# First attention of a two-layer decoder: projections of batches 1 to 3 from high and low parts, expert up weights loaded after them

## What is computed

```python
q = jnp.einsum('bsf,hfd->bhsd', x, wq)
k = jnp.einsum('bsf,hfd->bhsd', x, wk)
v = jnp.einsum('bsf,hfd->bhsd', x, wv)
scores = jnp.einsum('bhsd,bhtd->bhst', q, k) * scale
attn = jax.nn.softmax(scores, axis=-1)
out = jnp.einsum('bhst,bhtd->bhsd', attn, v)
feats = out.transpose(0, 2, 1, 3).reshape(x.shape[0], x.shape[1], H * DK)
return feats @ wo
...
x = x + _L0_attn_ref(_layernorm(x, axis=-1), L0_attn_wq, L0_attn_wk, L0_attn_wv, L0_attn_wo)
```

## Time and profile before

| | us |
|---|---|
| median of 3 runs | 1380.44 (1379.09 to 1383.38) |
| profiled execution | 1377.93 |
| its span, first to last instruction | 1376.0 |
| PE busy | 1247.9 (91%) |
| DVE busy | 980.6 (71%) |
| ACT busy | 710.2 (52%) |
| POOL busy | 622.6 (45%) |
| chain that ended last, on PE | 67% |

### The profile page before, as it was taken

How to read it: one execution, slowest core, us unless ns; L and a number is a source line. 1 busy time by engine, 2 the same in 40 slices (tenths; PEclk the granted TensorE clock), 3 DMA queues, 4 the chain that set the end, 5 groups by cost and what they waited for, 6 DMA issues and landing times.

```text
span 1376.0 us, 29293 instructions
## 1 busy us (share of the span) xinstructions
PE 1247.9 (91%) x10862; PEld 913.7 (66%) x10862; DVE 980.6 (71%) x2360; ACT 710.2 (52%) x1471; POOL 622.6 (45%) x770
## 2 busy tenths in 40 slices
PE   7999999999999989842669989989999999989998
PEld 5667667667776756530347656767777777777887
DVE  5988897787788778678313467677878888776554
ACT  4566666666666646510113345556666666633222
POOL 3555555555555521120631368685555755401110
PEclk9999999999999999965879989999999999999999
DMA  5131000000000020000023134211120211000001
GB/s 179 55 124 32 1 2 1 1 1 1 1 1 1 1 70 2 1 1 0 11 65 98 37 73 119 41 49 30 38 57 20 56 38 29 4 1 1 0 0 30
DMA packets 77000, 43.87 MB, mean 32 GB/s; under 512 B 26090, under 2 KB 71739, under 8 KB 76871
## 3 DMA queue, kind: packets, MB, share of 16 engines
q1 hardware_dynamic: 72390, 38.58, 10.6%
q10 hardware_dynamic: 2432, 2.28, 0.5%
q0 software_dynamic: 2048, 1.27, 0.4%
HBM read 21.89 MB, written 10.49 MB: 24 GB/s over the span
## 4 chain that ended last, share of the span: by engine, by line
PE 67%; DVE 16%; ACT 5%; issue 4%; POOL 4%; SPq 2%; DMA 1%; POOLq 0%; DVEq 0%; ACTq 0%
PE psum L1670 8%; PE psum L1270 7%; PE psum L1779 6%; PE psum L1255 6%; PE psum L1245 6%; PE psum L1790 4%; PE psum L1682 4%; PE psum L1654 4%; PE psum L1661 3%; PE psum L1502 3%; ACT arena L895 2%; PE psum L1221 2%; POOL xs_rows L666 2%; PE psum L1512 2%; DVE arena L2187 2%
## 5 line engine op out<-in xcount | busy, mean ns | idle before, releaser
L614 POOL TENSOR_TENSOR arena<-arena,rden 128x512 f32<-128x512 f32 x256 | 260.6, 1042 | 215.1 <-DVE rden L1925 215.0
L895 ACT ACTIVATE arena<-psum,negmax 128x512 f32<-128x512 f32 x256 | 175.1, 694 | 151.0 <-DVE negmax L1916 124.1
L2458 DVE TENSOR_REDUCE negmax<-psum 128x1 f32<-128x512 f32 x256 | 164.6, 685 | 50.4 <-PE psum L1661 48.3
L1916 DVE TENSOR_REDUCE negmax<-psum 128x1 f32<-128x512 f32 x256 | 168.1, 681 | 40.2 <-PE psum L1245 39.0
L1255 PEld LDWEIGHTS psum<-cst,arena 128*128 128x128 f32 x1024 | 112.6, 141 | 47.4 <-issue 46.8
L1255 PE MATMUL psum<-cst,arena 128*128 128x128 f32 x1024 | 139.3, 277 | 4.4 <-DVE arena L1911 0.8
L1245 PE MATMUL psum<-a_qk 64*128 64x512 f32 x768 | 106.1, 408 | 2.5 <-DVE a_qk L1934 2.5
L1779 PE MATMUL psum<-f_h,f_w 128*128 128x512 f32 x384 | 100.3, 410 | 7.1 <-DVE arena L2556 6.9
L1654 PE MATMUL psum<-a_kstack,a_qblk 96*128 96x512 f32 x256 | 96.9, 460 | 9.9 <-DMA a_kstack<-a_klo 7.4
L1149 ACT ACTIVATE arena<-psum 128x512 f32<-128x512 f32 x64 | 38.1, 597 | 107.5 <-PE psum L1779 107.5
L1245 PEld LDWEIGHTS psum<-a_qk 64*128 64x128 f32 x768 | 67.2, 184 | 39.1 <-issue 24.2
(11 more groups left out here) (342 smaller groups left out, 2722.3 us busy)
## 6 DMA issues: line engine op xcount, KB each, us to landing
w<-in_ew SPq DMA_DIRECT2D x2, 2048.0 KB, 9.5
a_kstack<-a_khi SPq DMA_DIRECT2D x64, 64.0 KB, 2.0
xs_rows<-f SPq DMA_DIRECT2D x3, 1024.0 KB, 5.3
arena<-xs_rows SPq DMA_DIRECT2D x8, 384.0 KB, 3.7
ys_rows<-wqkv SPq DMA_DIRECT2D x8, 384.0 KB, 2.6
a_kstack<-a_klo SPq DMA_DIRECT2D x32, 64.0 KB, 2.0
a_kstack<-a_khi SPq DMA_DIRECT2D x64, 32.0 KB, 1.9
a_qstack<-a_qhi SPq DMA_DIRECT2D x121, 16.0 KB, 2.7
```

Of the source, the lines that this page charges most:

```text
L614: pool.tensor_tensor(a0_p[u % 4], a0_p[u % 4], rden[:, u:u + 1].broadcast_to([P, SEQ]), ALU.mult).then_inc(a0_norm, 1)
L895: act.activation(a0_p[u % 4], bank[u % 4][:, :], ACT.Exp, bias=negmax[:, u:u + 1], accum_out=den[:, u:u + 1]).then_inc(a0_exp, 1)
L1916: dve.tensor_reduce(negmax[:, u:u + 1], bank[u % 4][:, :], AX.X, ALU.max, negate=True).then_inc(a0_max, 1)
L2458: dve.tensor_reduce(negmax[:, n % 8:n % 8 + 1], bank[n % 4][:, :], AX.X, ALU.max, negate=True).then_inc(a1_max, 1)
```

## The change

For batches 1 to 3 each projection becomes three fp32r products that are summed in PSUM: high weights by high tokens, high weights by low tokens, low weights by high tokens. Batch 0 stays as it was.

- The parts of the weights, `wq_hi` and `wq_lo` for all three projections of one pair, are made by two POOL operations of 128x384 after the eight multiplications of turns 1 to 8.
- The high tokens are what ACT writes in `turned_tokens` for batches 1 to 3 (the same operation, with fp32r as its output type). The low tokens are a new DVE operation of 128x512, `a0_low_tokens`, in the first half of turns 4, 7 and 10, between the maxima of steps 1 and 2. PE's output product of those turns waits for it.
- The query and key projections are three matmuls of 512 columns in place of one fp32 product. The value projection is twelve matmuls of 128 columns, each with its own 128x128 weights, in place of four fp32 products.
- The parts lie in `w13` (and over `hT`), so the up weights are loaded after the last value projection. `load_a1` moves from the eighth place between the turns to the fifth.

```diff
+        tok_hi = over("a0_hhi", [P, TOK], "hT", 0)
+        wq_hi = over("a0_whi", [P, 3, H * DK], "w13", 0)
+        wq_lo = over("a0_wlo", [P, 3, H * DK], "w13", 3 * H * DK)
+        tok_lo = over("a0_hlo", [P, (B - 1) * SEQ], "w13", 6 * H * DK)
...
-            between = [lambda: zero_rows(0), lambda: zero_rows(1), lambda: zero_rows(2), load_gate, lambda: load_up(0),
-                       lambda: load_up(1), load_shared_up, load_a1]
+            between = [lambda: zero_rows(0), lambda: zero_rows(1), lambda: zero_rows(2), load_gate, load_a1]
...
+            sp.wait_ge(a0_v, PAIRS)
+            load_shared_up()
+            for w in range(2):
+                load_up(w)
             sp.wait_ge(a0_pv, 2 * PAIRS)
...
+            def split_projections(pair):
+                cols = slice(pair * P, (pair + 1) * P)
+                chained(pool.tensor_tensor(wq_hi[:, :, cols], wqkv[:, :, cols], bcast(ones[:, :], 1, 3), ALU.mult))
+                chained(pool.tensor_tensor(wq_lo[:, :, cols], wqkv[:, :, cols], wq_hi[:, :, cols].bitcast(F32), ALU.subtract))
+
             for g in range(PAIRS):
+                if g == 1:
+                    pool.wait_ge(ld_a0, 64)
...
+                if 1 <= g <= HP:
+                    split_projections(g - 1)
...
-                act.activation(hT[:, b * SEQ:(b + 1) * SEQ], bank[7 if n else 4][:, :], ACT.Copy).then_inc(ln_out, 1)
+                act.activation((tok_hi if 1 <= n < B else hT)[:, b * SEQ:(b + 1) * SEQ], bank[7 if n else 4][:, :], ACT.Copy).then_inc(ln_out, 1)
...
+            def a0_project(g, i, o):
+                b, cols = g // HP, slice(g % HP * P, (g % HP + 1) * P)
+                if b == 0:
+                    return pe.matmul(o[:, :], wqkv[:, i, cols], hT[:, 0:SEQ], start=True, stop=True)
+                if i == 0 and g % HP == 0:
+                    pe.wait_ge(pre_dve, 4 + b)
+                if i == 0 and b == 1:
+                    pe.wait_ge(ln_pool, 2 * (g % HP) + 2)
+                high, low = tok_hi[:, b * SEQ:(b + 1) * SEQ], tok_lo[:, (b - 1) * SEQ:b * SEQ]
+                pe.matmul(o[:, :], wq_hi[:, i, cols], high, start=True, stop=False)
+                pe.matmul(o[:, :], wq_hi[:, i, cols], low, start=False, stop=False)
+                return pe.matmul(o[:, :], wq_lo[:, i, cols], high, start=False, stop=True)
...
                 for kt in range(QT):
-                    mm = pe.matmul(bank[6][:, kt * P:(kt + 1) * P], hT[:, (g // HP * QT + kt) * P:(g // HP * QT + kt + 1) * P],
-                                   wqkv[:, 2, g % HP * P:(g % HP + 1) * P], start=True, stop=True)
+                    o, t = bank[6][:, kt * P:(kt + 1) * P], b * QT + kt
+                    if b == 0:
+                        mm = pe.matmul(o, hT[:, t * P:(t + 1) * P], wqkv[:, 2, cols], start=True, stop=True)
+                    else:
+                        pe.matmul(o, tok_hi[:, t * P:(t + 1) * P], wq_hi[:, 2, cols], start=True, stop=False)
+                        pe.matmul(o, tok_hi[:, t * P:(t + 1) * P], wq_lo[:, 2, cols], start=False, stop=False)
+                        mm = pe.matmul(o, tok_lo[:, (t - QT) * P:(t - QT + 1) * P], wq_hi[:, 2, cols], start=False, stop=True)
...
                     pe.wait_ge(ln_out, A0 * B + NORM_TURN[g + 2] + 1)
+                    if NORM_TURN[g + 2] < B:
+                        pe.wait_ge(pre_dve, 4 + NORM_TURN[g + 2])
...
+            def a0_low_tokens(n):
+                dve.wait_ge(ln_out, A0 * B + n + 1)
+                dve.tensor_tensor(tok_lo[:, (n - 1) * SEQ:n * SEQ], bank[7][:, :], tok_hi[:, n * SEQ:(n + 1) * SEQ].bitcast(F32),
+                                  ALU.subtract).then_inc(pre_dve, 1)
+
             def a0_first_half(g):
                 a0_maximum(g, 0)
                 a0_maximum(g, 1)
+                if g in NORM_TURN and NORM_TURN[g] < B:
+                    a0_low_tokens(NORM_TURN[g])
```

More of the change, by code:

```diff
@@ L609, in _, with chained @@
             pool.memset(x0_one[:, 3 * HD:4 * HD], 1.0).then_inc(x0_ones, 1)
+            linked = [0]
+            def chained(ins):
+                linked[0] += 1
+                ins.then_inc(ln_pool, 1)
+                pool.wait_ge(ln_pool, linked[0])
+            def split_projections(pair):
+                cols = slice(pair * P, (pair + 1) * P)
+                chained(pool.tensor_tensor(wq_hi[:, :, cols], wqkv[:, :, cols], bcast(ones[:, :], 1, 3), ALU.mult))
+                chained(pool.tensor_tensor(wq_lo[:, :, cols], wqkv[:, :, cols], wq_hi[:, :, cols].bitcast(F32), ALU.subtract))
             for g in range(PAIRS):
+                if g == 1:
+                    pool.wait_ge(ld_a0, 64)
                 for u in range(UN):
@@ L619, in _ @@
                                        ALU.mult).then_inc(pre_pool, 1)
-            linked = [0]
-            def chained(ins):
-                linked[0] += 1
-                ins.then_inc(ln_pool, 1)
-                pool.wait_ge(ln_pool, linked[0])
+                if 1 <= g <= HP:
+                    split_projections(g - 1)
             def batch_norm(b, scales, h):
@@ L1220, in a0_project_q @@
                     pe.wait_ge(a0_vc, g)
-                pe.matmul(bank[6 if g else 5][:, :], wqkv[:, 0, g % HP * P:(g % HP + 1) * P], hT[:, g // HP * SEQ:(g // HP + 1) * SEQ],
-                          start=True, stop=True).then_inc(a0_q, 1)
+                a0_project(g, 0, bank[6 if g else 5]).then_inc(a0_q, 1)
             def a0_project_k(g):
@@ L1226, in a0_project_k @@
                     pe.wait_ge(a0_ql, g + 1)
-                pe.matmul(bank[6][:, :], wqkv[:, 1, g % HP * P:(g % HP + 1) * P], hT[:, g // HP * SEQ:(g // HP + 1) * SEQ],
-                          start=True, stop=True).then_inc(a0_k, 1)
+                a0_project(g, 1, bank[6]).then_inc(a0_k, 1)
             def a0_project_v(g):
                 pe.wait_ge(a0_kl, g + 1)
+                b, cols = g // HP, slice(g % HP * P, (g % HP + 1) * P)
                 for kt in range(QT):
-                    mm = pe.matmul(bank[6][:, kt * P:(kt + 1) * P], hT[:, (g // HP * QT + kt) * P:(g // HP * QT + kt + 1) * P],
-                                   wqkv[:, 2, g % HP * P:(g % HP + 1) * P], start=True, stop=True)
+                    o, t = bank[6][:, kt * P:(kt + 1) * P], b * QT + kt
[5 more added lines that the diff above has]
+                        mm = pe.matmul(o, tok_lo[:, (t - QT) * P:(t - QT + 1) * P], wq_hi[:, 2, cols], start=False, stop=True)
                 mm.then_inc(a0_v, 1)
```

## The result

The changed kernel takes 1386.49 us in the median of 20 runs (1381.6 to 1393.1), the kernel before 1380.47 in 20 runs of its own; the ratio is 1.0045, with a 95% interval of 1.0033 to 1.0056. Forecast were 1387.3 us and a slower kernel.

The account below looks back on a forecast made before the run. PE was taken to bound the first attention, with DVE and ACT leading in some turns. Values +7.0, queries -3.3, keys 0, POOL's splits +2.9 and low tokens +0.3 made +6.9 us on 1380.44: 1387.3 us, range 1380.5 to 1392.

Parts of the forecast that it names:

- Values, +0.44 a turn: Value projection on PE: twelve matmuls paced by weight loads take 1.33 us for 0.89; 7.0 us lost in 16 undisturbed turns.
- Queries, -0.165 kept 20 times: Query projection on PE: 0.70 us for 0.86, kept in 16 undisturbed turns and four disturbed ones, 3.3 us gained.
- Keys, nothing kept: Key projection on PE: 0.165 us shorter, but the transposes behind wait for ACT's copy of step 1; 0 gained.
- POOL's splits, +2.9: Ends of turns 2, 5, 7, 8: POOL's new operations hold DVE's SBUF-only operations, 2.9 us lost (0 to 3.6).
- meets the second split: Ends of turns 5 and 8: DVE's second operation of line 1901 is held by POOL's second split; up to +1.2 us.
- slips in between: Ends of turns 5 and 8: DVE's second operation of line 1901 gets in between POOL's two splits; +0.53 us.
- Low tokens, +0.3: Turns 4, 7 and 10: three DVE operations of 0.69 us cost 0.1 us each, 0.3 in all (0 to 1.5).
- Disturbed turns swallow the values' growth: Turns 8, 9, 11, 12, 19, 20, 27, 28: the value projection's +0.44 us disappears in a wait on PE; 0.
- The sign that I had named: Sign of a right prediction: the first halves of turns 11 and 12 stay as long as before.
- Loads, 0: The two 2 MB loads, now starting at some 470 us, are in by 500, needed after 540; cost 0.
- The sum: Whole kernel: 7.0 - 3.3 + 0 + 2.9 + 0.3 = +6.9 us, 1387.3 us on the median.
- narrow fp32r at the cost of fp32: Rival for the value projection: each 128-column product takes two records, 2.68 us; +37 us, 1417 us; chance 0.12.

Follow-up runs that it names:

- value_plain: Changed kernel with values back in four plain fp32 products: 445.24 us from turn 1 to turn 31's second half (changed 452.74), whole-time ratio 0.9976 to the kernel before.
- value_wide: Changed kernel with its twelve value products over 256 columns in place of 128: products 0.120 us apart, undisturbed first half 8.39 us, from 8.29.
- query_plain: Changed kernel with only the query projection back in one plain fp32 product: turn 1 to turn 31's second half 456.15 us, 3.41 us longer.
- the swap on ACT: Changed kernel with ACT's copy of step 1 ahead of its exponential of step 4: undisturbed second halves 6.06 us, turn 1 to turn 31's second half 454.52 us.
- key_one: Changed kernel with one product of high parts in place of three for keys: turn 1 to turn 31's second half 452.69 us (changed 452.74).
- key_one_swap: Changed kernel with one key product and ACT's step 1 copy ahead of its step 4 exponential: second halves 6.00 us, turn 1 to turn 31's second half 453.65.
- splits_alone: Kernel before with late up weights and POOL's sixteen splits, their parts unread: turn 1 to turn 31's second half 449.47 us, 4.39 over late loads alone; ratio 1.0029.
- loads_late: Kernel before with the experts' up weights loaded after the last value projection: turn 1 to turn 31's second half 445.08 us (before 445.26), ratio 0.9990.

## Why the prediction was right, point by point

- **Values, +0.44 a turn.** Right, by 1.29 us in the chain, loads 0.112 apart, and 7.07 us taken back by value_plain in the sixteen turns (7.0 forecast). The row that decided it was one of products of eight columns: it gave the price of a load where the price of the product was not to be had. value_wide shows that it is the load that counts and not the columns.
- **Queries, -0.165 kept 20 times.** Right: 3.41 us by query_plain.
- **Keys, nothing kept.** Nearly: 0.54 us in all, 0.03 a turn. The reason was right as far as it went, shown by the swap on ACT, but it left out DVE's copy of step 0, which is the limit as soon as the keys get shorter still (key_one, and the 6.00 of key_one_swap).
- **POOL's splits, +2.9.** The mechanism was right and the size too small: 4.4 us by splits_alone. Two terms were mis-sized. The operation takes 1.00 us, not 0.83, which I had set between two shapes without a row of its own. And of the pairs at the ends of turns 5 and 8 I took the mean (0.85) of "meets the second split" and "slips in between"; it meets it each time, +1.4. POOL pauses 0.08 us between its two splits, and that let none of these pairs in between. The prediction also has small slips that change no conclusion: 135.43 - 134.83 is 0.60, not 0.63, and 60.48 + 0.83 is 61.31, which makes 0.49 for turn 3, not 0.58.
- **Low tokens, +0.3.** Too dear: turns 4, 7 and 10 show only what queries and values explain (8.44, 8.28 and 8.72 from 8.45, 8.45 and 8.44). In turn 7 the low tokens are done at 123.45 and PE's output product, which waits for them, starts at 123.69. That ACT's exponentials had half a microsecond to spare fits, but no run takes the low tokens away alone.
- **Disturbed turns swallow the values' growth.** Nearly: value_plain takes 0.14 out of each of the three later pairs of turns, where two value pieces in the open would be 0.88. The pairs gave -0.18 each in all. One query's gain is 0.165, but the terms behind it are 0.18 gained by the queries (query_plain), 0.14 lost by the values and some 0.14 gained elsewhere, which no run separates. The sign that I had named, first halves of turns 11 and 12 as long as before, did not come: they fell from 8.45 and 8.69 to 8.32 and 8.30, and the second half between them grew from 6.29 to 6.65.
- **Loads, 0.** Right in the first attention, by loads_late, and no wait for them shows behind it.
- **The sum.** +6.9 forecast, +7.48 in the profiled turns, +6.0 in the medians. That the median moved by less than the turns is within the interval of the ratio (4.6 to 7.7 us). I have no cause for it. In all seven timed kernels, which all load late, the ratio lies lower than the stretch alone would say, by 0.2 to 3.3 us; with late loads alone the interval is 3.7 us to either side, so a small gain of the late loads in the rest of the program is neither shown nor excluded. The mechanisms were right, but that 1387.3 lies within 1 us of the median is in part luck: the splits were put 1.5 us too low, low tokens and keys 0.8 too high, and the whole program came out 1.5 under its turns.
- **A rival's sum.** In that of narrow fp32r at the cost of fp32 the last term, 1.4, has no source; with the 2.9 and 0.3 of the forecast it comes to +39 us. The rival is out in any case: the twelve products take one record each, 1.29 us and not 2.68.

## What to carry to other kernels

Three fp32r products pay in place of one fp32 product only where each streams many columns past its weights: at 512 columns 0.70 for 0.86 us, at 128 columns 1.33 for 0.89, because every product brings a load of its own, and loads came no closer than 0.11 us apart with 8 or with 128 columns behind them. That POOL has room does not make it free to prepare the parts there: put such operations where DVE has nothing that touches SBUF alone, and count two in a row as held twice. And a shorter piece on PE gains only as far as the next copy of its inputs is ahead: look which engine's order sets that copy, and swap it only in those turns where that engine is not itself the path.

## What the runs showed of the hardware

The timeline of PE gives for an fp32r product with new weights 0.112 us at 128 columns, 0.120 at 256 and 0.2325 at 512: nearly flat up to 256, and at 512 about the 0.213 of 512 columns at 2.4 GHz. And the granted clock fell to 1.2 GHz for some 6 us in the middle of a stretch with PE busy throughout, in one execution and not in another over the same 23 matmuls. Such a fall moved this profile by 3.1 us (the lag of 5.4 to 8.5), and among the 20 runs of the changed kernel those with a mean clock lower by 0.001 were on average 0.9 us longer. POOL's operations are not timed by columns alone: 308 took 0.71 us, 384 as three times 128 into fp32r 1.00, 512 took 1.04.
